# One attention and ternary feed-forward kernel: every engine's order of a step rewritten around the two Hadamard products

## Time and profile before

| what | value |
|---|---|
| median of three runs | 871.18 us |
| profiled execution | 873.74 us |
| its span, first to last instruction | 871.9 us |
| mean granted TensorE clock | 0.977 |
| PE busy | 797.4 us (91%) |
| PEld busy | 681.0 us (78%) |
| DVE busy | 661.9 us (76%) |
| ACT busy | 376.2 us (43%) |
| POOL busy | 266.9 us (31%) |

### The profile page before, as it was taken

One profiled execution on the slowest core, in us unless ns is written; L12 is line 12 of the kernel. 1 busy time (PEld: TensorE's weight loads), 2 busy tenths in 40 slices (PEclk: granted clock), 3 DMA queues, 4 the chain that ended last, 5 costly groups with the idle time before them and its releaser, 6 DMA issues.

```text
span 871.9 us, 19069 instructions
## 1 busy us (share of the span) xinstructions
PE 797.4 (91%) x7625; PEld 681.0 (78%) x7625; DVE 661.9 (76%) x1243; ACT 376.2 (43%) x687; POOL 266.9 (31%) x324
## 2 busy tenths in 40 slices
PE   6965899999999999999999999999999999998777
PEld 4855788888888888888888888888888888786563
DVE  3455777887788778877788788877887788777864
ACT  1564245444433444444434454444334444443321
POOL 1202332333233333333233323332333333322311
PEclk8968999999999999999999999999999999999989
DMA  8521111111111101111111011111111110000000
GB/s 276 171 97 31 29 30 33 41 43 44 44 44 31 39 30 32 43 44 44 43 36 36 30 31 44 43 44 43 44 30 34 34 34 26 28 26 27 13 12 13
DMA packets 38285, 39.65 MB, mean 45 GB/s; under 512 B 21172, under 2 KB 22324, under 8 KB 38196
## 3 DMA queue, kind: packets, MB, share of 16 engines
q1 hardware_dynamic: 34436, 33.48, 12.5%
q10 hardware_dynamic: 3760, 4.95, 1.7%
HBM read 30.02 MB, written 8.39 MB: 44 GB/s over the span
## 4 chain that ended last, share of the span: by engine, by line
PE 59%; DVE 17%; POOL 10%; ACT 7%; issue 6%; ACTq 1%; DMA 1%; POOLq 0%; DVEq 0%
PE bank L322 35%; DVE hid L223 13%; POOL gT L223 9%; PE bank L499 8%; PE bank L442 7%; PE bank L412 4%; PE bank L520 3%; ACT hid L660 2%; ACT hid L658 2%; ACT gT L683 2%; PE bank L430 1%; DMA k_bd<-in_L_attn_Wk_dram 1%; ACTq L598 1%; DVE s L761 0%; DVE srow L765 0%
## 5 line engine op out<-in xcount | busy, mean ns | idle before, releaser
L223 DVE TENSOR_TENSOR hid<-hid 128x256 f32<-128x256 f32 (+1 forms) x192 | 136.1, 748 | 5.6 <-ACT hid L660 0.9
L223 POOL TENSOR_TENSOR hid<-hid 128x256 f32<-128x256 f32 x128 | 100.0, 801 | 118.4 <-DVE hid L860 115.9
L223 POOL TENSOR_TENSOR gT<-gT 128x256 f32<-128x256 f32 x124 | 87.7, 729 | 157.2 <-ACT gT L683 154.8
L499 PE MATMUL bank<-cst_sb,hid 128*128 128x128 f32 x512 | 68.5, 289 | 25.6 <-DVE hid L223 25.6
L499 PEld LDWEIGHTS bank<-cst_sb,hid 128*128 128x128 f32 x512 | 62.2, 198 | 31.8 <-DVE hid L223 31.8
L939 POOL TENSOR_TENSOR s<-s,srow 128x512 f32<-128x512 f32 x32 | 33.5, 1046 | 172.2 <-DVE srow L782 164.5
L322 PE MATMUL bank<-h_hi,wk_hi 128*128 128x256 f32 x256 | 77.4, 303 | 9.0 <-ACT v_bd L566 5.3
L678 ACT ACTIVATE late<-bank,sc 128x1024 f32<-128x1024 f32 x32 | 35.8, 1117 | 98.1 <-DVE sc L895 98.1
L918 POOL TENSOR_TENSOR h_lo<-h_sum,h_hi 128x512 fp32r<-128x512 f32 x32 | 41.0, 1285 | 113.0 <-ACT h_hi L553 105.7
L322 PE MATMUL bank<-h_hi,wq_hi 128*128 128x256 f32 x256 | 75.4, 295 | 0.0
L322 PE MATMUL bank<-h_lo,wk_hi 128*128 128x256 f32 x256 | 73.1, 286 | 0.0
(11 more groups left out here) (114 smaller groups left out, 2004.7 us busy)
## 6 DMA issues: line engine op xcount, KB each, us to landing
x_in<-in_x_dram SPq DMA_DIRECT2D x32, 256.0 KB, 2.8
x_res<-in_x_dram SPq DMA_DIRECT2D x32, 256.0 KB, 2.6
out_dram<-late SPq DMA_DIRECT2D x32, 256.0 KB, 3.1
w_bd<-in_L_cond_weights_dram SPq DMA_DIRECT2D x126, 16.0 KB, 2.0
bias_in<-in_fside_8xS_dram SPq DMA_DIRECT2D x62, 32.0 KB, 2.9
k_bd<-in_L_attn_Wk_dram ACTq DMA_DIRECT2D x1, 1024.0 KB, 5.5
s<-in_L_attn_Wq_dram ACTq DMA_DIRECT2D x1, 1024.0 KB, 8.4
v_bd<-in_L_attn_Wv_dram ACTq DMA_DIRECT2D x1, 1024.0 KB, 10.7
```

What stands on the lines that cost most here:

```text
L223: eng.tensor_tensor(dv[:, :, n], sv[:, :, 0], sv[:, :, 1], op).then_inc(done, 1)
L499: mm = pe.matmul(ps01[:, m * P:(m + 1) * P], hid[:, 1, m, :], had, start=True, stop=True)
```

## The change

The functions of a step are named (`scores`, `qk`, `hadamard1`, `turn_q1`, and so on) and called in a new order on every engine. The arithmetic and the count of matmuls stay.

- TensorE: scores, qk 1, qk 2, first Hadamard, v, transposes of q2 of pair c-2, cond1 of c+4, down of c-2, transposes of q1, transposes of P, qk 3, P v, up, o, qk 4, cond2, second Hadamard. The second Hadamard product is now the last of the step, and its quantisation falls into the next one.
- VectorE: it begins a step with the scale of the second quantisation (`scale2`), and rounds q2 in the middle of the softmax. It does all of hid's butterflies (the first stage in two halves, then second and third over all eight chunks), and no longer the square of hid's first half, the copy of pT's first half, or the normalise of the second half.
- GpSimd: gT's butterflies stand at the head of the following step, and it normalises both halves of P. It does no butterflies of hid.
- ScalarE: squares both halves, copies both halves of pT, in a new order.
- The product of the two first scales (sc2's column 1) moves to the first quantisation's group.
- PSUM: the second Hadamard writes banks 4 and 5 (`ps45`), over up; scores keep banks 0 and 1 and share them with the turned P; the first Hadamard and cond2 go to bank 6, beside P v; the turned q1 goes to bank 5 and the turned q2 to bank 4; cond1 has bank 7 alone.
- SyncE: the loads of cond1 for pair c+6 are issued ahead of the store and of cond2's loads.

The core of the diff:

```diff
+            def hadamard2(f):
+                for m in range(FC):
+                    if m % 4 == 0:
+                        pe.wait_ge(d_had, f * 8 + 7 + m // 4)
+                    mm = pe.matmul(ps45[:, m * P:(m + 1) * P], hid[:, 1, m, :], had, start=True, stop=True)
+                mm.then_inc(s_f2, 1)
...
+            def down(c):
+                pe.wait_ge(d_q2t, c - 1)
+                pe.wait_ge(a_qk, jobs_done(c, 1))
...
+                if attn:
+                    scores(c)
+                if nxt:
+                    qk(c, 0, 0)
+                    qk(c, 1, 1)
+                if ffn:
+                    hadamard1(c - 1)
+                if attn:
+                    v_product(c)
                 if c == NPAIR:
                     keep_clock(10, up_w[:, 0, :])
+                if fin:
+                    turn_q2(c - 2)
+                if cnd:
+                    pe.wait_ge(s_cin1[c % 2], (c // 2 + 3) * 80)
+                    pe.wait_ge(d_h, c + AHEAD)
+                    cond1(c + AHEAD)
+                if fin:
+                    down(c)
+                if ffn:
+                    turn_q1(c - 1)
+                if attn:
+                    turn_p(c)
                 if nxt:
+                    qk(c, 2, 4)
+                if attn:
+                    pv(c)
+                if ffn:
+                    up(c - 1)
+                if attn:
+                    o_product(c)
+                if nxt:
+                    qk(c, 3, 6)
+                if attn:
+                    cond2(c)
                 if c == NPAIR:
                     keep_clock(18, up_w[:, 0, :])
                 if ffn:
+                    hadamard2(c - 1)
+                if c == NPAIR:
+                    keep_clock(18, up_w[:, 0, :])
...
+                if nxt:
+                    copy_next_qk(c, 0, 0)
+                if fin:
+                    act.wait_ge(d_q2, (f - 1) * 5 + 4)
+                    act.activation(y2, ps45[:, :], ACT.Copy, bias=MAGIC, scale=sc2[:, 4:5]).then_inc(a_y2, 1)
+                if nxt:
+                    copy_next_qk(c, 1, 1)
+                if attn and c + 1 < NPAIR:
+                    if c % 2 == 1:
+                        act.wait_ge(a_qk, jobs_done(c - 1, 3))
+                    spread_k(c + 1)
+                if attn:
+                    exp(c, 0)
                 if c == 0:
                     w_round(0, 0)
                 if ffn:
+                    act.wait_ge(d_q1, f * 6 + 4)
+                    act.activation(y1[:, :], bank[6], ACT.Copy, bias=MAGIC, scale=sc1[:, 3:4]).then_inc(a_y1, 1)
+                if attn:
+                    exp(c, 1)
+                    if c == 0:
+                        act.wait_ge(s_vbd_zero, 1)
+                    copy_v(c)
                 if c == 0:
                     w_round(0, 1)
+                if cnd:
+                    copy_hi(c + AHEAD)
+                if attn:
+                    copy_pt(c, 0)
+                    copy_pt(c, 1)
                 if nxt:
+                    copy_next_qk(c, 2, 4)
+                if attn:
+                    act.wait_ge(s_pv, c + 1)
                     act.activation(oT_hi[:].rearrange("p a b -> p (a b)"), bank[6], ACT.Copy).then_inc(a_ohi, 1)
                 if c == 0:
                     w_abs_sum(1, 0)
                     w_abs_sum(1, 1)
+                if c == 1:
+                    act.wait_ge(s_fclip, 4)
+                if ffn:
+                    relu_square(f, 0)
+                    relu_square(f, 1)
                 if nxt:
+                    copy_next_qk(c, 3, 6)
+                if attn:
+                    act.wait_ge(s_g, c + 1)
+                    act.activation(gT[:].rearrange("p a b -> p (a b)"), bank[6], ACT.Copy).then_inc(a_g, 1)
...
+            def scale1_back(f):
+                dve.tensor_scalar(sc1[:, 4:5], sc1[:, 1:2], wsum[:, 0, 3:4], 1.0 / QB, ALU.mult, ALU.mult).then_inc(d_q1, 1)
+                dve.wait_ge(d_q1, f * 6 + 5)
+                dve.tensor_scalar(sc2[:, 1:2], sc1[:, 4:5], sc1[:, 4:5], FF ** -0.5, ALU.mult, ALU.mult).then_inc(d_q1, 1)
...
+            def round1(f):
+                dve.wait_ge(a_y1, f + 1)
+                dve.tensor_scalar(q1[:, :], y1[:, :], MAGIC, QB, ALU.subtract, ALU.min).then_inc(d_q1c, 1)
...
+                    scale2(f - 1)
                 if c == NPAIR:
+                    dve.wait_ge(a_g, c)
                     butterflies(dve, gT[:], gT2[:], 0, d_g)
                     dve.wait_ge(d_g, 2)
                     butterflies(dve, gT2[:], gT[:], 1, d_g)
                 if attn:
+                    add_alibi(c, 0)
+                    row_max(c, 0)
+                    add_alibi(c, 1)
+                    less_max(c, 0)
                 if fin:
+                    round2(f - 1)
+                if c == 0:
+                    w_scale(0)
+                if attn:
+                    row_max(c, 1)
+                if ffn:
+                    scale1_max(f)
+                if attn:
+                    less_max(c, 1)
+                if ffn:
+                    scale1(f)
+                if attn:
+                    exp_sum(c, 0)
+                if ffn:
+                    scale1_back(f)
+                    round1(f)
+                if fin:
+                    copy_q2t(f - 1)
+                if attn:
+                    exp_sum(c, 1)
                 if c == 1:
                     clip_low(1, 0)
                     clip_low(1, 1)
+                    clip_high(1)
                 if c == 0:
                     clip_low(0, 0)
                     clip_low(0, 1)
+                    clip_high(0)
                 if cnd:
+                    dve.wait_ge(p_hlo, c + 3)
+                    add_bias(c + AHEAD)
+                if fin:
+                    add_out(c)
+                if ffn:
+                    copy_q1t(f)
+                if attn:
+                    split_o(c)
+                if ffn:
+                    dve.wait_ge(a_sq, 2 * f + 1)
+                    butterflies(dve, hid[:, 0, 0:4], hid[:, 1, 0:4], 0, d_had)
+                    dve.wait_ge(a_sq, 2 * f + 2)
+                    butterflies(dve, hid[:, 0, 4:8], hid[:, 1, 4:8], 0, d_had)
+                    dve.wait_ge(d_had, 8 * f + 4)
+                    butterflies(dve, hid[:, 1], hid[:, 0], 1, d_had)
+                if attn:
+                    add_x(c)
+                if ffn:
+                    dve.wait_ge(d_had, 8 * f + 6)
+                    butterflies(dve, hid[:, 0], hid[:, 1], 2, d_had)
...
+                if attn and ffn:
+                    pool.wait_ge(a_g, c)
+                    butterflies(pool, gT[:], gT2[:], 0, p_g)
+                    pool.wait_ge(p_g, c * 4 - 2)
+                    butterflies(pool, gT2[:], gT[:], 1, p_g)
+                if attn:
+                    normalize(c, 0)
+                    normalize(c, 1)
```

More of the change, by code:

```diff
@@ new lines, in o_product, with cond2 @@
+            def o_product(c):
+                pe.wait_ge(a_ohi, c + 1)
+                pe.wait_ge(d_olo, c + 1)
+                if c >= 2:
+                    pe.wait_ge(d_out, c - 1)
+                else:
+                    pe.wait_ge(a_qk, jobs_done(c, 1))
+                w, o = (w_hi["wo"], w_lo["wo"]), (oT_hi, oT_lo)
+                split_product(ring(c, 5), lambda a, k: o[a][:, k, :], lambda b, k: w[b][:, k, :]).then_inc(s_wo, 1)
+            def cond2(c):
+                pe.wait_ge(d_x1, c + 1)
+                for m in range(KC):
+                    mm = pe.matmul(bank[6][:, m * P:(m + 1) * P], x1[:, c % 2, m * P:(m + 1) * P],
+                                   w2_bd[:, c % 2, :], start=True, stop=True)
+                mm.then_inc(s_g, 1)
@@ new lines, in up @@
+            def up(f):
+                pe.wait_ge(d_q1t, f + 1)
+                if f == 0:
+                    pe.wait_ge(s_fready, 2)
+                for m in range(FC):
+                    dst = bank[4 + m // 4][:, (m % 4) * P:(m % 4 + 1) * P]
+                    for k in range(KC):
+                        mm = pe.matmul(dst, up_w[:, k, m * P:(m + 1) * P], q1T[:, k, :],
+                                       start=(k == 0), stop=(k == KC - 1))
+                    if m % 4 == 3:
+                        mm.then_inc(s_up, 1)
@@ L346, in _ @@
+            def down(c):
+                pe.wait_ge(d_q2t, c - 1)
+                pe.wait_ge(a_qk, jobs_done(c, 1))
+                if c == 2:
+                    pe.wait_ge(s_fready, 4)
+                for k in range(FC):
+                    mm = pe.matmul(ring(c, 3), q2T[:, k, :], down_w[:, k, :], start=(k == 0), stop=(k == FC - 1))
+                mm.then_inc(s_down, 1)
             pe.wait_ge(s_bd_zero, 2)
@@ L599, in _ @@
                               by_row_half[:, r]).then_inc(s_cst, 16)
-            for c in range(2):
-                copy_hi(c, c)
+            copy_hi(0)
+            copy_hi(1)
             split_w("wq")
@@ L616, in _ @@
                 if job in (5, 6):
```

(20 more changed lines are left out.)

580 lines of the change are left out of this document (211 added, 369 removed).

## The result

The changed kernel takes 891.12 us (median of four runs, 890.6 to 892.82) against 871.25 for the kernel before on the same occasion. The ratio is 1.0232, with a 95% interval of 1.0214 to 1.0249: it is slower by 2.3%. The forecast was 890.

A forecast was written before the change was run, and what follows sets the result against it. TensorE bound the kernel, computing 47.63 of 49.52 us. Span 871.9 + 11.5 (28 steps at +0.41) + 1 (start) + 6 (tail) = 890.4; plus 1.8 around the span, less 2.56, gave 890 us, own range 882 to 900.

The forecast's parts named there:

- The term that decided: On VectorE, round1 waits for the rest of GpSimd's first-half normalise, to 9.74, and ends at 10.02, 0.69 us later.
- rival (a): round1 and GpSimd's normalise hardly meet: step 24.48, 870 us, between 863 and 879; chance 0.18.
- The queue on VectorE: VectorE's work from the second Hadamard's end: scale2, softmax, round1 reached at 8.91, q2T's copy ending at 10.64 us.
- the wait: TensorE stands ready for down at 9.14 but starts it at 10.69, a wait of 1.55 us for q2T.
- the 0.19 at cond2: cond2 starts 6.30 after up, where TensorE would be at 6.11, and costs the step 0.19 us.
- the start: Step 1's cost from weight clips ahead of copy_q1t and the pT copies: +1 us, bounds -2 and +5.
- both forecast effects: In step 1, clips delay copy_q1t, add_bias and the pT copies; against it, a qk job precedes the first Hadamard.
- the tail: Steps 30, 31 and the drain: spells of half clock after idle time, +6 us together, bounds +3 and +10.
- The correction of -2.56: The runs' median lies 2.56 us below the earlier kernel's profiled execution of 873.74, so 892.2 becomes 890.
- (b): TensorE becomes dense if VectorE delivers q2T by +9.14: step 23.43 to 23.6, about 842 us; chance 0.09.
- (c): The 1.5 us wait lets the clock fall inside the steady run: +35 if every second step, 925 us; chance 0.06.
- (d): ScalarE's pT copies come 1.0 us later than counted, moving pv by 0.4 to 0.5 a step: 903 us; chance 0.08.

The follow-up runs named there:

- e2: Changed kernel with GpSimd's normalise of the first half also waiting for round1, so the two cannot run together; 865.4 us, ratio 0.9914.
- e8: Changed kernel with only x1 moved, between the two operations of hid's second stage on VectorE; 887.61 us, ratio 1.0171.
- e3: Changed kernel with 18 extra matmuls, results unused, ahead of the down product in steps 30 and 31; 887.57 us, ratio 1.0173.
- e4: Changed kernel with copy_q2t and second exp_sum ahead of round1, x1 earlier, P's transposes ahead of q1's, pT copies ahead of copy_hi; 837.86 us.
- e11: Changed kernel with only ScalarE's pT copies moved ahead of copy_hi; 890.99 us, ratio 1.0220.
- e6: Changed kernel with copy_q2t and second exp_sum ahead of scale1_back and round1 on VectorE, and P's transposes ahead of q1's on TensorE; 855.04 us.
- e1: Changed kernel with one swap on VectorE, copy_q2t ahead of round1; 859.28 us, ratio 0.9855.

## Why the prediction was right

**The term that decided.** The forecast let round1 wait for the rest of GpSimd's normalise and end 0.28 behind it; it ends 0.29 behind it, in 1.16 us. It was put 0.69 later, and is 0.74 later; its 1.16 us lie just above the 0.8 to 1.1 that the forecast named as its sign. e2 takes this away and gives 0.75 a step (25.10 to 24.35); rival (a), the kernel without the meeting, was given 870, and e2 measured 865.4. The Trainium skill's "SBUF — State Buffer", section "Who interferes with whom", has a VectorE operation in a two-port mode, which a tensor_scalar can enter, and a GpSimd operation exclude each other for the whole instruction, and the traces agree for round1: 0.42 alone, 1.16 when it starts 0.17 into the normalise, 0.56 when it starts 0.76 into one of 1.04.

**The queue on VectorE.** Round1 was reckoned at 8.91 from the scores and stands at 8.68; q2T's copy was to end at 10.64 and ends at 10.44. The 0.23 at round1 lies almost all at the head of the queue: scale2 took 1.96 from its start to the alibi's where I had 2.04 (my own terms, 1.90 + 0.13 - 0.1, make 1.93), and it started at +0.11 in place of +0.24, since the second Hadamard ends closer to the scores than in the earlier trace rows.

**TensorE.** To down 9.03 against 9.14, and the wait 1.5 from start to start against 1.55 (the row's 1.25 leaves out the pipeline's end). From down to the next scores 14.60 against 14.48, with the 0.19 at cond2 in it: cond2 starts 6.30 after up, as worked out, and e8 returns the 0.19. Most of the 0.12 too little is cond2 itself, 0.99 from start to start where I had 0.89. The step came out at 25.10 against 25.17, so 28 steps gave +9.8 where the sum had +11.5.

**Start and end.** The two terms here were the weak ones, and they missed in opposite directions. For the start I took +1, and it was -1.9, near the bound. The traces take it apart in part. 1.05 of the 1.9 lies ahead of step 1; e3, whose start is the same code, gained 1.2 in all where the changed kernel gained 1.9, so some of it is the difference between two executions. In step 1 both forecast effects are there: with a qk job done before it, the first Hadamard waits 6.15 us for gT in place of 8.15, and P v, whose pT copies stand behind the clips, waits 2.64:

```profile
88.67 1.15 PE L369 MATMUL bank<-pT,v_bd 128*64 128x64 f32 x32 [2.64 <-issue]
```

For the tail I took +6 with a bound of +10, and it was +9.0: both idle spells of 4.1 us were followed by half clock, as said. Step 30 took 2.6 us more than before, the stretch from the scores of step 31 to the first Hadamard of the drain 1.5 more, and the stretch from there to the drain's second Hadamard 5.0 more (16.58 in place of 11.56; the first two rows are the kernel before, the third is the changed one, whose first Hadamard starts at 859.68):

```profile
847.64 1.05 PE L412 MATMUL bank<-cst_sb,gT 128*128 128x128 f32 x8
...
859.20 2.05 PE L499 MATMUL bank<-cst_sb,hid 128*128 128x128 f32 x16 [1.20 <-DVE hid L223]
...
876.26 2.05 PE L425 MATMUL bank<-cst_sb,hid 128*128 128x128 f32 x16 [0.56 <-DVE hid L215]
```

With the filler of e3 the 2.6 becomes 0.9 and the 1.5 becomes -0.8, but 4.2 of the 5.0 stay. In that stretch the new order has the transposes of q2 and down, which the old one ran ahead of it. The forecast priced the tail as spells of half clock and had no term for this. The sum was 890.4 for a span of 888.8, and that it is so near is luck in part: the start was 2.9 too high and the tail 3.0 too low. The correction of -2.56 from the profiled execution to the median has no counterpart either, for the changed kernel's profiled execution lies 0.5 below its median.

**The rivals.** (b) fell as forecast by the argument that VectorE's queue is too long even without the block: e2 still waits 0.52. But its price, "about 842", came close for the kernel in which the queue is shortened: e4 is at 837.9. (c) did not happen in the steady run (granted clock 1.00), but behind the longer wait of steps 28 and 29 it did in three of the runs, and cost 1.6 us a step there. (d), late pT copies, is refuted for the changed kernel by e11 and holds in e6.

What stays open: no run moves down or the transposes in the drain, so the 4.2 us there are located but not tested; where the start won the 1.05 ahead of step 1; and why a wait of 2.2 us is followed by half clock in one execution and not in another.

## What to carry to other kernels

When an order is rewritten to make the busiest engine dense, walk the second engine's queue from the last event it waits for to the operand that the first engine needs next; here that queue was 1.5 us too long, and one swap in it (e1) was worth 32 us, more than the change had lost. Then lay the GpSimd operations beside it: a VectorE tensor_scalar from SBUF to SBUF that starts behind a GpSimd operation pays the rest of it (round1 here; the earlier trace rows has the same of a tensor_tensor with two SBUF inputs), so put there what these runs show unharmed, the tensor_scalar that reads PSUM or the tensor_reduce, or one that nobody waits for. A move is worth something only where the wait is: the pT copies alone were worth nothing in e11, while in e6 P v waits for them.

## What the runs showed of the hardware

- The block works in both directions. In step 0 of the changed kernel VectorE's pair of bf16 tensor_scalars took 2.98 us in place of 1.29, and GpSimd's two normalises beside it 1.55 and 1.48 us (3.00 together), where one took 1.04 in the steady step:

```profile
50.62 3.00 POOL L884 TENSOR_TENSOR s<-s,srow 128x512 f32<-128x512 f32 x2 [7.01 <-issue]
...
51.19 2.98 DVE L701 TENSOR_SCALAR up_w<-up_w 128x2048 bf16<-128x2048 bf16 x2
```

- A tensor_scalar with its source in PSUM (q2T's copy, 0.68 to 0.69) and a tensor_reduce from SBUF (L723, 0.68 in e2) are not slowed beside the same GpSimd operation.
- A wait of 2.2 us ahead of down, in steps 28 and 29, was followed by a granted clock of 0.50 in one execution (e8) and not in another (the changed kernel, 1.00 from 763 to 767 us), with the same order of work on TensorE ahead of it.
